# Both layers of the kernel in one program stretch: the second layer's first group is loaded, mixed and split at the end of the mixing layer

## What is computed

```
xn = layernorm(x)
x  = x + scanned(xn) @ w2.T + b2 + quantised(xn) @ quantised(W).T + bias   # layer 0
xn = layernorm(x)
# layer 1, attention: q, k = relu(xn @ Wq.T + bq), relu(xn @ Wk.T + bk); v = xn @ Wv.T + bv
# kv = sum over tokens of k (x) v, per head;  k_sum = sum of k
# out = layernorm((q @ kv) / (q . k_sum) + xn) * gamma + beta
# layer 1, channel mixing, with prev = xn one token earlier:
# r = sigmoid((mu_r*xn + (1-mu_r)*prev) @ W_r)
# k = relu((mu_k*xn + (1-mu_k)*prev) @ W_k) ** 2;  ff = r * (k @ W_v)
x  = x + out + ff
```

## Time and profile before

| | us |
|---|---|
| median of 3 runs | 2141.53 (2141.03 to 2142.42) |
| the profiled execution | 2144.58 |
| its span (first to last instruction) | 2142.8 |
| PE busy in the span | 2089.7 |
| mixing phase, steps 3 to 63 | to 1314.6 |
| last instruction of the first block | 1355.0 |
| first matmul of the second layer | 1369.68 |

### The profile page before, as it was taken

One profiled execution on the slowest core, in us unless ns is written; L12 is line 12 of the kernel. 1 busy time (PEld: TensorE's weight loads), 2 busy tenths in 40 slices (PEclk: granted clock), 3 DMA queues, 4 the chain that ended last, 5 costly groups with the idle time before them and its releaser, 6 DMA issues. The chain is left out here.

```text
span 2142.8 us, 27599 instructions
## 1 busy us (share of the span) xinstructions
PE 2089.7 (98%) x9466; PEld 1672.6 (78%) x9466; DVE 1471.6 (69%) x2884; ACT 1092.9 (51%) x1834; POOL 839.6 (39%) x844
## 2 busy tenths in 40 slices
PE   7999999999999999999999999699999999999998
PEld 6888888544578888888888887478888888888887
DVE  4776555576687777776777773476667776767776
ACT  4554555423355555555555553456554455555543
POOL 1021000255454545454444542044445443443454
PEclk9999999999999999999999999799999999999999
DMA  4333533776533333333333330422222222222211
GB/s 151 118 128 138 159 118 109 247 257 218 189 115 106 120 105 113 119 108 99 125 131 122 105 113 35 147 66 81 91 69 69 69 69 90 88 99 69 69 40 40
DMA packets 174838, 241.40 MB, mean 113 GB/s; under 512 B 19049, under 2 KB 109417, under 8 KB 173930
## 3 DMA queue, kind: packets, MB, share of 16 engines
q1 hardware_dynamic: 161576, 216.10, 30.6%
q10 hardware_dynamic: 13122, 23.53, 3.0%
HBM read 138.86 MB, written 100.73 MB: 112 GB/s over the span
## 5 line engine op out<-in xcount | busy, mean ns | idle before, releaser
L99 PE MATMUL bank<-e_ring,e_w_hi 128*128 128x512 f32 x512 | 202.6, 396 | 16.7 <-DVE e_ring L1681 16.7
L100 PE MATMUL bank<-e_ring,e_w_hi 128*128 128x512 f32 x512 | 200.7, 392 | 0.0
L101 PE MATMUL bank<-e_ring,e_w_lo 128*128 128x512 f32 x512 | 200.5, 392 | 0.0
L1315 PE MATMUL bank<-d_kh,d_nat 128*128 128x512 f32 x768 | 192.8, 400 | 5.5 <-DVE d_kh L1181 5.5
L1555 POOL TENSOR_TENSOR e_x<-e_x,e_beta 128x512 f32<-128x512 f32 x64 | 91.5, 1448 | 230.8 <-ACT e_y L1596 230.7
L987 POOL TENSOR_TENSOR rstd<-d_var_eps,neg_half 128x1 f32<-128x1 f32 x64 | 35.6, 556 | 345.7 <-DVE d_var_eps L1201 345.7
L1315 PEld LDWEIGHTS bank<-d_kh,d_nat 128*128 128x128 f32 x768 | 140.1, 189 | 33.7 <-issue 6.7
L1603 ACT ACTIVATE e_kr<-bank 128x512 f32<-128x512 f32 x64 | 37.9, 592 | 239.3 <-PE bank L101 239.3
L1681 DVE TENSOR_TENSOR e_ring<-e_mixed,e_ring 128x512 fp32r<-128x512 f32 x128 | 93.3, 729 | 92.1 <-ACT e_ring L1574 92.1
L1535 POOL TENSOR_TENSOR e_x<-e_x,e_ff 128x512 f32<-128x512 f32 x64 | 83.3, 1302 | 177.1 <-DVE e_ff L1735 177.1
L1206 DVE TENSOR_TENSOR d_nat<-d_xn,d_nat 128x512 fp32r<-128x512 f32 x64 | 85.8, 1343 | 77.1 <-ACT d_nat L1088 77.1
(11 more groups left out here) (209 smaller groups left out, 6292.6 us busy)
## 6 DMA issues: line engine op xcount, KB each, us to landing
scr_v<-b_vt SPq DMA_DIRECT2D x64, 256.0 KB, 2.6
scr_z<-b_zt SPq DMA_DIRECT2D x64, 256.0 KB, 2.1
c_z<-scr_z SPq DMA_DIRECT2D x64, 256.0 KB, 4.0
...
e_xt<-scr_xnt SPq DMA_DIRECT2D x16, 1024.0 KB, 5.7
```

Source lines behind the costliest of these rows:

```text
L99: eng.matmul(out, lhs[hi], rhs[hi], start=first, stop=False, skip_group_check=onto)
L100: eng.matmul(out, lhs[hi], rhs[lo], start=False, stop=False, skip_group_check=onto)
L101: return eng.matmul(out, lhs[lo], rhs[hi], start=False, stop=last, skip_group_check=onto)
L1315: mm = pe.matmul(BG[c][:, :], s[:, i, cols], r[:, j, :], start=M % NTB == 0 and i == j, stop=M % NTB == NTB - 1 and i == 1, skip_group_che ...
```

## The change

All four phases are one block (`run_phases(nc, "two_layers", ...)`); the wait of all engines for each other is gone. Every tile of the second layer lies over a named tile of the mixing phase (`over`), and each first write waits for the last use of what was there (`keep["mix"]`).

- SP loads the turned tokens of group 0 in step 63, W_k at step 40, Wq after the last `forward`, W_r after the last `keys`, and the rest after the last `outer`.
- Steps 64 to 66 are written out by hand. On PE `keys(62)` goes to bank BB, opened by one more matmul (`open_bank`), and stands ahead of `outer(61)`, `keys(63)` ahead of `outer(62)`. On ACT and DVE the mixing of group 0 stands between the copies of these steps.
- The split of W_k lies in steps 50 to 54, that of Wq at the end of the tail.
- The first two of group 0's four banks of W_k products (`keys_out`) stand between `sums_row`, `values` and `sums_column` of the second half.
- At the start of the mixing phase `gate(2)`, `high_u(2)`, `low_u(2)` and `low_u(3)` stand earlier.

```diff
+    def keys_bank(M):
+
+        return BB if M == NT - 2 else BK
+
...
@@ -929,6 +947,8 @@
                 sp.wait_ge(x2_full, N + 1)
                 sp.wait_ge(gated, N // 2 + 2)
                 load_u(N // 2 + 2)
+            if N == NT - 1:
+                keep["layer"]["load_turned"](0)
...
-                i = (N - 40) // 2
-                sp.dma_start(ahead["raw"][i][:, :, :], ins[ahead["names"][i]]).then_inc(ahead["in"][i], 16)
-        for q in range(Q):
...
-            sp.wait_ge(ahead["in"][i], 16)
+            if N == 40:
+                keep["layer"]["load_weight"](0)
+            if N == NT - 1:
+                sp.wait_ge(x2_full, NT)
+                keep["layer"]["load_weight"](1)
 
     def finish_quantising(N):
         tile = xq[N % 3]
...
         low_u(1)
         root(1)
...
+        low_u(2)
         finish_quantising(4)
         add_keys(0)
-        low_u(2)
         root(3)
         finish_quantising(5)
-        for N in range(FILL + 1, NT + 3):
+        for N in range(FILL + 1, NT):
             add_keys(N - 3)
-            if N < NT:
-                root(N)
-            if N % 2 and N // 2 + 1 < NT // 2:
+            if N == FILL + 2:
+                low_u(3)
+            root(N)
+            if N > FILL + 2 and N % 2 and N // 2 + 1 < NT // 2:
                 low_u(N // 2 + 1)
             if N + 2 < NT:
                 finish_quantising(N + 2)
+        keep["layer"]["clear_edge"](0)
+        for M in range(NT - 3, NT):
+            add_keys(M)
 
...
-        if M:
-            act.wait_ge(k_lo, M)
+        if M == 0:
+            act.wait_ge(bank_open, 2)
+        elif M == NT - 2:
+            act.wait_ge(bank_open, 3)
         else:
-            act.wait_ge(bank_open, 2)
-        nc.scalar.activation(BK[:, :], bk[:, :], ACT.Copy).then_inc(k_set, 1)
+            act.wait_ge(k_lo, M if M < NT - 1 else NT - 2)
+        nc.scalar.activation(keys_bank(M)[:, :], bk[:, :], ACT.Copy).then_inc(k_set, 1)
...
         high_q(3)
+        high_u(2)
         normalise_sums(2)
...
-        for N in range(FILL, NT + 3):
...
+        for N in range(FILL, NT):
             keys(N - 3)
-            if N - 2 < NT:
-                set_keys(N - 2)
-            if N % 2 and N // 2 + 1 < NT // 2:
+            set_keys(N - 2)
+            if N > FILL and N % 2 and N // 2 + 1 < NT // 2:
                 high_u(N // 2 + 1)
...
+            if WEIGHT_HIGH_AT <= N < WEIGHT_HIGH_AT + KT:
+                keep["layer"]["weight_high"](0, N - WEIGHT_HIGH_AT)
+
+        layer = keep["layer"]
+        set_keys(NT - 2)
+        layer["previous"](0)
+        layer["previous"](1)
+        keys(NT - 3)
+        take_turned(NT - 1)
+        set_keys(NT - 1)
+        layer["mix_high"](0)
+        layer["mix_high"](1)
+        layer["previous"](2)
+        layer["previous"](3)
+        keys(NT - 2)
+        layer["mix_high"](2)
+        layer["mix_high"](3)
+        keys(NT - 1)
+        for kt in range(KT):
+            layer["plain_high"](kt)
+        for kt in range(KT):
+            layer["weight_high"](1, kt)
+        take_products(B - 1)
 
...
         low_n(0)
+        gate(2)
...
         low_nat(2)
-        gate(2)
-        for N in range(FILL, NT + 3):
+        for N in range(FILL, NT):
...
+            low_nat(N)
+            if N == WEIGHT_HIGH_AT:
+                keep["layer"]["set_rests"]()
+            if WEIGHT_LOW_AT <= N < WEIGHT_LOW_AT + KT:
+                keep["layer"]["weight_low"](0, N - WEIGHT_LOW_AT)
+
+        layer = keep["layer"]
+        layer["mix_sum"](0)
+        layer["mix_sum"](1)
+        low_keys(NT - 3)
+        low_n(NT - 1)
+        layer["mix_low"](0)
+        layer["mix_low"](1)
+        layer["mix_sum"](2)
+        low_keys(NT - 2)
+        layer["mix_sum"](3)
+        layer["mix_low"](2)
+        layer["mix_low"](3)
+        low_keys(NT - 1)
+        for kt in range(KT):
+            layer["plain_low"](kt)
         sums_row(B - 1)
+        for kt in range(KT):
+            layer["weight_low"](1, kt)
         values(B - 1)
         sums_column(B - 1)
 
...
+            if N == NT - 1:
+                open_bank(keys_bank(NT - 2))
...
+
+        turn_sums(NT - 1)
+        keys(NT - 2)
+        outer(NT - 3)
+        keys(NT - 1)
+        outer(NT - 2)
+        outer(NT - 1)
+        pe.wait_ge(n_lo, NT)
         sums_row(B - 1)
+        keep["layer"]["keys_out"](0)
         values(B - 1)
+        keep["layer"]["keys_out"](1)
         sums_column(B - 1)
 
     return (sync, gpsimd, vector, scalar, tensor), mix
...
+    WEIGHT = 4 * KT * D
+    w_hi_t = [ahead["hi"]] + [over(tile, f"e_w_hi{i}", [P, KT, D], F32R)
+                              for i, tile in ((1, "d_w2"), (2, "d_wk"), (3, "d_xt0"))]
+    lows = ((1, "d_w2", WEIGHT), (2, "d_wk", WEIGHT), (3, "d_gt", 0))
+    w_lo_t = [ahead["lo"]] + [over(tile, f"e_w_lo{i}", [P, KT, D], F32R, skip) for i, tile, skip in lows]
+    w_raw = [ahead["raw"]] + [over(tile, f"e_w_raw{i}", [P, KT, D], F32, skip) for i, tile, skip in lows]
...
+    ROW = 4 * D
+    x2 = [over("d_nat0", f"e_x2{i}", [P, GT, D], F32, i * GT * ROW) for i in range(2)]
+    xt = [over(tile, f"e_xt{i}", [P, KT, NCB + GN]) for i, tile in enumerate(("d_xq0", "d_kh0"))]
+    ring = [over(tile, f"e_ring{i}", [P, 2, KT, GN], F32R) for i, tile in enumerate(("d_ut0", "d_wf"))]
+    prev = [over("d_v0", f"e_prev{i}", [P, GN], F32, i * ROW) for i in range(2)]
+    mixed = [over("d_v1", f"e_mixed{i}", [P, GN], F32, i * ROW) for i in range(2)]
...
-    KQB, RVB, CB = banks[0:4], banks[4:6], banks[6:8]
+    KQB, RVB, CB = [banks[i] for i in (2, 1, 3, 0)], banks[4:6], banks[6:8]
+    bank_free = ("sums", "front_keys", "keys", "state")
...
+    def load_turned(g):
+        h, b, q = g % 2, g // NGB, g % NGB
+        columns = scr["xnt"].rearrange("(k p) t -> p k t", p=P)
+        if g == 0:
+            for s, n in [front["q_turned"], front["biases_read"]] + front["xnt_front"]:
+                sp.wait_ge(s, n)
+        if g >= 2:
...
 
...
-        load_turned(0)
-        for i in (2, 3):
-            sp.dma_start(w_raw[i][:, :, :], ins[ahead["names"][i]]).then_inc(w_in[i], 16)
+        sp.wait_ge(*front["keys_made"])
+        load_weight(2)
+        for s, n in [front["outer"], front["added"]] + front["x2_stored"] + front["xnt_stored"]:
+            sp.wait_ge(s, n)
         load(0)
         load_turned(1)
+        sp.wait_ge(*front["values"])
+        load_weight(3)
...
+    def clear_edge(b):
+
+        if b == 0:
+            pool.wait_ge(*front["q_turned"])
+            pool.wait_ge(*front["biases_read"])
+        else:
+            pool.wait_ge(mix_done, 8 * (NGB - 1))
+        nc.gpsimd.memset(xt[0][:, :, 0:1], 0.0).then_inc(edge, 1)
...
+            for m in range(KT):
+                if g or m >= 2:
+                    channels_out(g, 0, h, wk, k_full, m)
+            for m in range(KT):
+                channels_out(g, 1, 1 - h, wq, q_full, m)
...
-    run_phases(nc, "first_layer", (project, scan, mix))
-    run_phase(nc, "second_layer", phase_second_layer(nc, sh, ins, scr, keep, banks,
-                                                     Stretch(nc, after_small, SBUF_END - 2 * weight), ahead))
+    layer = phase_second_layer(nc, sh, ins, scr, keep, banks, mix_areas, ahead)
+    run_phases(nc, "two_layers", (project, scan, mix, layer))
```

357 lines of the change are left out of this document (172 added, 185 removed).

## The result

The changed kernel takes 2111.81 us (median of 4 runs, 2110.56 to 2113.2), the kernel before 2141.98 on the same chip: ratio 0.9858, 95% interval 0.9846 to 0.987. The forecast was 2107.3: the sign and the range of 2102.5 to 2114 held, the point was 4.5 us too low, and the result lies outside the forecast's own range of 2105 to 2110.

The account below looks back on a forecast made before the run. PE, busy 2089.7 of 2142.8 us, was taken as the bound. Gains of 32.8 us at the seam and 1.4 at the start of mixing make 34.2: 2141.53 - 34.2 = 2107.3 us, range 2102.5 to 2114, own range 2105 to 2110.

Parts of the forecast that it names:

- The sum on PE: Seam, last full step to first W_r matmul: PE's work is 50.1 us instead of 82.9, gaining 32.8.
- No new wait in the tail: Last steps before the second layer: ACT and DVE deliver 0.8 to 1.9 us before PE wants it; priced at nothing.
- rival 1: Tail: covers too thin, late pieces or a late landing lose 3 to 7 us, 2110 to 2114; chance 0.17.
- a lost cover: Tail: margin before PE wants a piece; if errors match the covers, one or two show 1 to 3 us each.
- The loads: Seam: group 0's turned tokens land 3 us before the first `prev`; W_v, issued at 1345, is there by 1360.
- Behind the seam: ACT's chain from the fourth W_k bank moves by the same 32.8 us; the 2.89 us first-gate wait stays.
- Rival 2: First gate of group 0: its 2.89 us stall and slow matmuls go if ACT gets ahead, some 5 us, 2102; chance 0.08.
- Rival 3: Seam: the 15.49 us were the load, not the block's end, and stay; 2123, up to 2131; chance 0.03.
- Rival 4: Second-layer groups: DVE's pieces stretch beside POOL until DVE is the bound; 2146 us; chance 0.03.
- Steps 50 to 54: Four ACT copies and four DVE splits added; what they delay is wanted a step later; price 0, bound 2.8 us.
- The start of the mixing phase: Earlier `low_u(2)` and `low_u(3)` remove PE waits of 1.05 and 1.39 us; 1.4 us gained, ends -0.7 and 2.4.
- the 1.39 go: Start of mixing: PE's 1.39 us wait for `low_u(3)` vanishes, as it now stands ahead of POOL's root of tile 5.

Follow-up runs that it names:

- mix_behind_keys: The changed kernel with group 0's mixing on ACT and DVE behind the last key copies instead of between them; 2123.97 us, ratio 0.9908.
- no_fillers: The changed kernel with both W_k banks of PE's tail behind `sums_column` instead of ahead of `values` and `sums_column`; 2117.71 us, ratio 0.9875.
- gate_chain_early: The changed kernel with the weight splits (W_r, W_v) of the first second-layer group moved into idle time of ACT and DVE; 2107.98 us, ratio 0.9835.
- joined: gate_chain_early with the old start order except `low_u(3)`, W_k's low parts ahead of `low_nat`, `again(0, 3)` and first `prev` behind the first gate; 2106.19 us.
- low_u3_early_only: The changed kernel with the old start order of the mixing phase, only `low_u(3)` ahead of the root of tile 5; 2110.46 us, ratio 0.9851.
- before_new_start: The kernel before with only the new start order of the mixing phase; 2144.08 us, ratio 1.0005.
- barrier_back: The changed kernel in two blocks again, all engines waiting between `sums_column` and the third W_k bank, group 0's preparation still ahead; 2117.06 us, ratio 0.9876.

## Why the prediction was right or wrong

- **The sum on PE: right.** 50.1 us foretold, 50.17 measured; 32.8 gained foretold, 32.73 measured. `sums_column` took the 0.95 us assumed.
- **No new wait in the tail: right**, and rival 1 wrong as a mechanism, though the time lies in its span of 2110 to 2114: there is no wait for `d_kh`, `e_ring` or `d_gt`. That the stated range of 2102.5 to 2114 held is therefore luck in part: it reached up to 2114 for rival 1, and the time was lost elsewhere. What a lost cover can cost was too low in it: in mix_behind_keys and no_fillers waits of 3.5 and 2.6 us made the seam 10.9 and 9.8 us longer, through the clock.
- **The loads: right.** No `prev` waits for a transfer. W_v came 5.4 us after its issue, not 14.8.
- **Behind the seam: right.** 0.77 and 2.89 us stayed, as the chain starts with the fourth bank. Rival 2 had the price right and the trigger wrong: it takes the splits out of the chain (gate_chain_early).
- **Rival 3: wrong**, the change does what it says; the barrier alone is 2.8 us of the seam and 2.6 behind it. **Rival 4: wrong**, PE is still busy for 47.00 of 47.00 us with DVE at 33.46.
- **Steps 50 to 54: priced at 0, cost 0.89 us.** The bound of 2.8 held. The step that failed is "what they could delay is wanted one step later": three of the four pieces take 1.77 us instead of 0.68, beside POOL's quantising (at 1178.85 and 1202.81 us) or its `add_keys` (at 1216.62), 6.0 us in all, and in step 55 POOL's root and `low_u`, which wait for DVE, are late. joined shows that the place in the step decides.
- **The start of the mixing phase: the term that failed.** +1.4 us foretold, with ends of -0.7 and +2.4; it was -1.65, outside both. Three parts of it: (1) "the 1.39 go" was wrong, they move to `low_u(4)` (low_u3_early_only); (2) the prediction saw that tile 4's quantising would come two to three us later "just when PE wants it" and priced that at 1.0 us (1.4 taken of the 2.4 for both stalls); it was a wait of 3.04 us for the 1.05 that went, and a gap at `turn_q(4)` is what the prediction itself named as a sign of being wrong; (3) behind that wait the clock falls, 1.0 us net, in four of the six profiles of the merged kernel with this order. The order by itself is worth -0.64 (before_new_start), just inside the ends.
- **The account of the miss:** 3.05 us at the start, 0.89 in steps 50 to 54, 0.15 in the seam and behind it, and 0.45 because the kernel before took 2141.98 and not 2141.53 us beside the changed one: 4.5.

What isn't settled: waits of 2.59, 2.73 and 2.98 us at `turn_q(4)` (gate_chain_early, before_new_start, barrier_back) left the clock at 1.00, and those of 3.04, 3.27, 3.27 and 3.31 us (the changed kernel twice, no_fillers, mix_behind_keys) didn't. Whether the length alone decides there isn't shown. Nor is it shown why one execution of no_fillers had a mean clock of 0.999 and another 0.993, or why the wait changed in length from one profile to the next under the same order.
